# A post-norm attention and mixture-of-experts layer on one core: shared down products moved into the last part, a router in four column groups, two steps moved to ScalarE, and a new order

## What is computed

```python
Q, K, V = (x @ W.T).reshape(b, s, h, hd)                  # h = 16, hd = 16
scores = einsum('bshd,bstd->bsht', Q, K) / sqrt(hd)       # heads of one token
x = layernorm(x + (softmax(scores) @ V).reshape(b, s, dm) @ Wfc.T)
scores = sigmoid(x @ router_weight.T); sfc = scores + router_bias
# 4 groups of 8 experts: best 2 groups by the sum of their top 2, then top 4 experts
topk_w = 2.5 * scores[topk_idx] / sum(scores[topk_idx])
mixed = sum_k topk_w[k] * (silu(x @ gate_w[e].T) * (x @ up_w[e].T)) @ down_w[e].T
shared = (silu(x @ sg.T) * (x @ su.T)) @ sd.T
x = layernorm(x + mixed + shared)
```

## Time and profile before

| | us |
|---|---|
| median of 3 runs | 721.03 |
| lowest, highest | 717.69, 722.21 |
| the profiled execution | 726.36 |
| its span, first to last instruction | 724.6 |
| first part, until PE transposes the first expert rows | 419.63 |
| last matmul of the expert loop starts | 656.97 |
| first picked rows added | 667.98 |

### The profile page before, as it was taken

How to read it: one execution, slowest core, us unless ns; L and a number is a source line. 1 busy time by engine, 2 the same in 40 slices (tenths; PEclk the granted TensorE clock), 3 DMA queues, 4 the chain that set the end, 5 groups by cost and what they waited for, 6 DMA issues and landing times.

```text
span 724.6 us, 16286 instructions
## 1 busy us (share of the span) xinstructions
PE 605.9 (84%) x4916; PEld 453.4 (63%) x4917; DVE 392.5 (54%) x1286; ACT 265.5 (37%) x521; POOL 290.1 (40%) x300
## 2 busy tenths in 40 slices
PE   6899998888597947578747989999999999993994
PEld 2366676565264625456524678788878888882883
DVE  2044675568056625368545446566565666562774
ACT  2344345334142502322212135455444555541224
POOL 4000003425327071516574316565556655554122
PEclk9999999789598977969776999999999999997899
DMA  6999968757237135859821224455445444444996
GB/s 225 270 223 250 238 187 236 174 163 214 99 109 220 45 126 181 323 180 382 286 106 67 90 71 148 133 144 157 147 133 154 150 159 158 148 153 153 417 411 238
DMA packets 125804, 135.34 MB, mean 187 GB/s; under 512 B 76856, under 2 KB 107071, under 8 KB 125120
## 3 DMA queue, kind: packets, MB, share of 16 engines
q1 hardware_dynamic: 108288, 95.92, 45.3%
q0 software_dynamic: 12672, 34.10, 12.5%
q10 hardware_dynamic: 4800, 4.74, 1.9%
HBM read 74.79 MB, written 60.96 MB: 187 GB/s over the span
## 4 chain that ended last, share of the span: by engine, by line
PE 15%; SPq 12%; issue 11%; DVE 6%; DMA 5%; another core or an unknown queue 2%; DVEq 1%; ACT 1%; POOL 0%; POOLq 0%; ACTq 0%
PE bank L868 14%; SPq L468 7%; SPq L470 5%; DMA wgu_sb<-pick_rows 3%; DMA prod<-expert_rows 2%; PE bank L1241 1%; DMA pick_rows<-prod,ids 1%; DVE prod L1709 1%; DVEq L250 0%; DVE prod L1733 0%; DVE bidx L1456 0%; DVE best L1453 0%; DVE gtop L1426 0%; SPq L474 0%
## 5 line engine op out<-in xcount | busy, mean ns | idle before, releaser
L527 POOL DMA_INDIRECT expert_rows<-stage,pos x128 | 127.2, 993 | 150.4 <-DVE pos L1393 80.4
L561 POOL DMA_INDIRECT pick_rows<-prod,ids x136 | 136.5, 1004 | 119.0 <-issue 51.8
L868 PE MATMUL bank<-prod 128*128 128x128 f32 x1088 | 134.4, 277 | 2.5 <-issue 1.3
L868 PEld LDWEIGHTS bank<-prod 128*128 128x128 f32 x1088 | 126.8, 192 | 5.7 <-issue 3.3
L868 PE MATMUL bank<-wgu_sb 128*32 128x64 f32 x2048 | 80.2, 297 | 50.3 <-issue 35.0
L868 PEld LDWEIGHTS bank<-wgu_sb 128*32 128x32 f32 x2048 | 64.5, 139 | 72.9 <-issue 59.2
L868 PE MATMUL bank<-wd_sb,wqkv_sb 128*128 128x512 f32 x192 | 92.8, 628 | 6.0 <-DMA wqkv_sb<-in_wqkv 6.0
L1709 DVE COPY prod<-wgu_sb 128x512 f32 x136 | 61.2, 491 | 63.0 <-issue 38.6
L827 ACT ACTIVATE prod<-bank,kept 128x256 f32<-128x256 f32 x136 | 57.1, 471 | 40.4 <-PE bank L868 21.9
L868 PE MATMUL bank<-wd_sb,prod 128*128 x272 | 70.3, 381 | 1.3 <-issue 0.8
L868 PEld LDWEIGHTS bank<-wd_sb,wqkv_sb 128*128 128x128 f32 x192 | 37.2, 201 | 46.3 <-issue 40.2
(11 more groups left out here) (138 smaller groups left out, 777.0 us busy)
## 6 DMA issues: line engine op xcount, KB each, us to landing
prod<-expert_rows SPq DMA_DIRECT2D x136, 132.0 KB
wgu_sb<-pick_rows SPq DMA_DIRECT2D x32, 512.0 KB, 14.1
wgu_sb<-in_wgu SPq DMA_DIRECT2D x2, 2560.0 KB
expert_rows<-pad_rows SPq DMA_DIRECT2D x4, 1056.0 KB
wd_sb<-in_xT SPq DMA_DIRECT2D x8, 512.0 KB, 4.3
q_slots<-wd_sb SPq DMA_DIRECT2D x16, 256.0 KB
k_slots<-wd_sb SPq DMA_DIRECT2D x16, 256.0 KB
wgu_sb<-q_slots SPq DMA_DIRECT2D x16, 256.0 KB
```

The source lines that it names most:

```text
L527: pool.indirect_dma_start(xs, bass.IndirectOffsetOnAxis(ap=pos[e % 2][:, i, k:k + 1], axis=0), stage[:, i, k, :], None, bounds_check=XROWS ...
L561: pool.indirect_dma_start(z, bass.IndirectOffsetOnAxis(ap=ids[par][:, j:j + 1], axis=0), y_sb[par][:, j, :], None, bounds_check=TOPK * NTO ...
L868: return pe.matmul(dst, lhsT, rhs, start=(k == 0), stop=(k == n - 1))
```

## The change

1. **Shared down products of chunks 5, 6 and 7** are taken out of the first part. `DOWN_AT_ONCE = 5` chunks keep them. PE does the other three after the expert loop, straight into the banks of the last sums, where x1 (without the shared product) and the picks are added. The last sums take the chunks in the order 5, 6, 7, 0, 1, 2, 3, 4. Chunk 7's `hsT` gets a third place, over the projection weights. DVE does no `add_shared` for these three.
2. **The router** holds its weights (32 columns) still and streams 128 tokens, with the four tiles in four groups of 32 columns of the array. The result is transposed, so ACT copies it (`copy_logits`) and PE turns it back with one transpose (`turn_logits`).
3. **ACT normalises** the first layer norm (from a negated mean that DVE computes, `negate_mean`) and **copies the counts** (`copy_ranks`).
4. **All five lists** get a new order; in it, waits for banks move along.

```diff
-COUNT_BANKS = (4, 4, 4, 4, 5, 7, 4, 4)
-DOWN_BANKS = ((5, 4), (5, 4), (7, 4), (5, 4), (5, 4), (5, 4), (5, 4), (5, 4))
+COUNT_BANKS = (4, 4, 4, 4, 4, 4, 4, 5)
+DOWN_BANKS = ((5, 4), (5, 4), (5, 6), (5, 4), (5, 4))
+DOWN_AT_ONCE = 5
+LAST_ORDER = (5, 6, 7, 0, 1, 2, 3, 4)
...
+        hsT_last = wqkv_sb.rearrange("p k c -> p (k c)")[:, 0:2 * CT].rearrange("p (k c) -> p k c", k=2)
+
+        def hs_of(b):
+            return hsT[b % 2] if b < DOWN_AT_ONCE + 2 else hsT_last
...
+        logT = eneg1
...
-        ones_e = sb("ones_e", [P, NE])
+        ones_e = over(prod, 25 * DM - NE, NE)
...
-                    at = (g * TPC + t) * P
+                    at = (LAST_ORDER[g] * TPC + t) * P
...
             invert(0)
             invert(1)
-            scatter_rows(0, 0, 8)
+            scatter_rows(0, 0, 5)
             invert(2)
...
+            scatter_rows(3, 6, 16)
+            scatter_rows(4, 0, 8)
             invert(6)
-            scatter_rows(4, 14, 16)
-            scatter_rows(5, 0, 3)
+            scatter_rows(4, 8, 16)
+            scatter_rows(5, 0, 9)
             invert(7)
...
+            def copy_logits(b):
+                act.wait_ge(S["logT_ready"], b + 1)
+                if b:
+                    act.wait_ge(S["onehot_ready"], b)
+                act.activation(logT[:, :], banks[LOGITS_BANK][:, 0:P], ACT.Copy).then_inc(S["logT_copied"], 1)
+
+            def normalise(b):
+                act.wait_ge(S["rstd_ready"], b + 1)
+                act.wait_ge(S["nmean_ready"], b + 1)
+                for i in range(TPC):
+                    act.activation(x1_of(b)[:, i, :], res[:, i, :], ACT.Identity, bias=nmeant[:, i:i + 1],
+                                   scale=rstdt[:, i:i + 1]).then_inc(S["x1_ready"], 1)
+
+            def copy_ranks(e):
+                act.wait_ge(S["rank_ready"], e + 1)
+                if e:
+                    act.wait_ge(S["rk"], RK * e)
+                act.activation(ranks_sb[:, :, :],
+                               banks[COUNT_BANKS[e]][:, 0:(TPC + 1) * NE].rearrange("p (i e) -> p i e", e=NE),
+                               ACT.Copy).then_inc(S["rk"], 1)
...
-                for i in range(TPC):
-                    for k in range(KC):
-                        last = mm(banks[LOGITS_BANK][:, i * NE:(i + 1) * NE],
-                                  x1T_sb[b % X1T][:, k, i * P:(i + 1) * P], wr_sb[:, k, :], k, KC)
-                last.then_inc(S["logits_ready"], 1)
+                for k in range(KC):
+                    for i in range(TPC):
+                        last = mm(banks[LOGITS_BANK][i * NE:(i + 1) * NE, 0:P], wr_sb[:, k, :],
+                                  x1T_sb[b % X1T][:, k, i * P:(i + 1) * P], k, KC)
+                last.then_inc(S["logT_ready"], 1)
+
+            def turn_logits(b):
+                pe.wait_ge(S["logT_copied"], b + 1)
+                pe.transpose(banks[LOGITS_BANK][:, P:2 * P], logT[:, :], ident[:, :])\
+                    .then_inc(S["logits_ready"], 1)
...
-            def normalise(b):
+            def negate_mean(b):
                 dve.wait_ge(S["rstd_ready"], b + 1)
-                for i in range(TPC):
-                    dve.tensor_scalar(x1_of(b)[:, i, :], res[:, i, :], mvt[:, i, 0:1], rstdt[:, i:i + 1],
-                                      ALU.subtract, ALU.mult).then_inc(S["x1_ready"], 1)
+                dve.scalar_tensor_tensor(out=nmeant[:, :], in0=mvt[:, :, 0], scalar=-1.0, in1=rstdt[:, :],
+                                         op0=ALU.mult, op1=ALU.mult).then_inc(S["nmean_ready"], 1)
...
+            def sum_down(g, b):
+                pe.wait_ge(S["hs_ready"], 2 * (b + 1))
+                for t in range(TPC):
+                    for k in range(2):
+                        pe.matmul(sum_of(g, t), hs_of(b)[:, k, t * P:(t + 1) * P], wsd_sb[:, k, :],
+                                  start=(k == 0 and t % 2 == 0), stop=False)
...
+            for g in range(CH - DOWN_AT_ONCE):
+                sum_down(g, LAST_ORDER[g])
+            for g in range(CH):
+                sum_rows(g, LAST_ORDER[g])
```

More of the change, by code:

```diff
@@ new lines, in _ @@
+            stage_rows(1, range(3, 4))
+            evacuate(6, 2)
+            normalise(3)
+            copy_o(4, 1)
+            evacuate(6, 3)
+            exponents(5, 0)
+            turned(3, 0)
+            evacuate(6, 4)
+            expand(5, 0)
+            copy_ranks(2)
+            stage_rows(2, range(0, 1))
+            exponents(5, 1)
+            tanh_of(0, 0)
+            stage_rows(2, range(1, 2))
+            turned(3, 1)
+            expand(5, 1)
+            copy_logits(3)
@@ new lines, in _ @@
+            evacuate(6, 5)
+            sigmoid_parts(3)
+            stage_rows(2, range(2, 3))
+            copy_o(5, 0)
+            exponents(6, 0)
+            stage_rows(2, range(3, 4))
+            normalise(4)
+            copy_o(5, 1)
+            evacuate(7, 0)
+            expand(6, 0)
+            evacuate(7, 1)
+            evacuate(7, 2)
+            exponents(6, 1)
+            copy_ranks(3)
+            evacuate(7, 3)
+            stage_rows(3, range(0, 2))
+            expand(6, 1)
@@ L771, in _ @@
+            copy_o(6, 0)
+            stage_rows(3, range(2, 3))
+            turned(4, 0)
+            tanh_of(0, 1)
+            turned(4, 1)
+            copy_o(6, 1)
+            copy_logits(4)
+            stage_rows(3, range(3, 4))
+            sigmoid_parts(4)
+            evacuate(7, 4)
+            tanh_of(1, 0)
+            evacuate(7, 5)
+            normalise(5)
+            exponents(7, 0)
+            tanh_of(1, 1)
             turned(5, 0)
-            tanh_of(1, 1)
+            stage_rows(4, range(0, 3))
@@ L1548, in _ @@
             moments_of(4)
+            route(3, 0)
+            shift(6, 0)
+            negate_mean(4)
+            route(3, 1)
             weights(6, 0)
-            normalise(4)
+            route(3, 2)
+            shift(6, 1)
+            route(3, 3)
+            weights(6, 1)
+            place(3)
+            gated(0, 1)
             residual(5, 0)
```

776 lines of the change are left out of this document (363 added, 413 removed).

## The result

The changed kernel took 758.65 us (median of 4 runs, 756.54 to 763.28) against 720.33 us for the kernel before: a ratio of 1.054, with a 95% interval of 1.048 to 1.060. I had predicted 699.

A forecast was written before the change was run, and what follows sets the result against it. No engine total bounds the kernel; before the loop, latency and waits do, with most hanging on POOL's scatter chain. Terms -6.7, -8 and -7, the rest 0, sum to -21.7: 726.4 to 704.7, less 5.3 to the median, 699 us (690 to 709).

The forecast's parts named there:

- B: Rival, chance 0.10: before the loop, two more pairs of small-matmul batches held up by scatters, 16.6 us each; 733 us.
- Term 1: At the loop's start: without the shared down products in front, the loop begins on the first loaded rows, -6.7 us.
- Term 2: Between loop and sums: the moved down products fill PE's 10.63 us of idling, 0 us (-3 to +10).
- Term 3: Router in four column groups: PE's gain against an added transpose, copy and hand-overs, 0 us (-8 to +5).
- Term 4: Normalising and count copies moved from DVE to ACT in the first part: 0 us (-9 to +4).
- Terms 5 and 6: First part's new order: less PE work before chunk 4's counts, -8 us; chunk 6's earlier projection halves POOL's 12.65 us hole, -7.
- rival A: Rival, chance 0.22: the part before the loop keeps its pace, only the tail's 6.7 us is gained, 714 us.

The follow-up runs named there:

- e5: The changed kernel itself, unaltered, run in the quiet condition: 611.4 us, ratio 0.961 to the kernel before.
- e3: The kernel before with the changed kernel's places in SBUF and its three more semaphores, unused, no instruction added: 639.0 us, ratio 1.001.
- e17: The changed kernel with 32 more instructions that do nothing on VectorE, crawling condition: 761.2 us, ratio 1.044 to the kernel before.
- e18: The changed kernel with the shared down products back in front of the loop and 24 more do-nothing VectorE instructions, crawling: 766.0 us, ratio 1.050.
- e4: The kernel before with only the shared down products of chunks 5 to 7 moved behind the loop, and the sums' chunk order: 638.7 us, ratio 1.002.
- e9: The changed kernel with the shared down products of chunks 5 to 7 back in front of the loop: 608.1 us, ratio 0.958 to the kernel before.
- e8: The changed kernel with the old router back: 616.8 us, ratio 0.971 to the kernel before.
- e7: The changed kernel with normalising and the copy of the counts back on VectorE: 626.3 us, ratio 0.983 to the kernel before.

## Why the prediction was wrong

**The step that failed** is the sentence that the change "rewrites the order of the first part and touches the loop not at all, so the question is when the loop can begin". The loop was in my sum with a difference of nothing and no bound. It was +39.6 us in the comparison, and -9.7 us in the quiet condition (e5 against e3). No rival covered it either; B put the slower case into the head. The evidence to be cautious stood in my own rows: GpSimd's scatters held up streams of instructions without a releaser, and the loop has 136 of them. I had also looked only for what the trace called crawling in the head; two pauses of 3.3 and 3.5 us stood in the loop.

**Term 1** (-6.7, down products behind the loop). In the crawling condition it was right: the loop began on the first loaded rows and no longer on these products. From the last scatter's end to the first transposes it takes 5.6 us instead of 12.2, so 6.6 of the head's 8.3 us are this term, and e17 against e18 gives 4.5. In the quiet condition it is worth nothing: e4 and e9 show no gain in the medians, since there the products fit beside the last scatters and row loads.

**Term 2** (0, -3 to +10). Right: +1.4 us to the first sum. The granted clock was 0.98 instead of 0.88, but the sums took as long as before (+0.1), so the 3 us that I had allowed for it did not come.

**Term 3** (0, -8 to +5). The new router is worth -6.5 us (e8), inside its bounds.

**Term 4** (0, -9 to +4). In the quiet condition ScalarE's share is worth -8.7 us in the head (e7), at the end of the range. In the comparison it may have cost instead. ACT pauses there while GpSimd scatters, and now holds normalising and staging, on which GpSimd waits. ACT and POOL of the changed kernel, crawling:

```profile
301.03 0.28 ACT L664 ACTIVATE eneg<-bank 128x128 f32<-128x128 f32 x1 [2.15 <-PE bank L990]
...
313.84 0.97 POOL L534 DMA_INDIRECT expert_rows<-stage,pos  x1 [0.30 <-issue]
316.41 1.04 ACT L631 ACTIVATE wgu_sb<-bank 128x512 f32<-128x512 f32 x1 [15.10 <-remote]
317.77 2.05 ACT L651 ACTIVATE sx<-prod,nmeant,rstdt 128x256 f32<-128x256 f32 x4
...
324.82 0.20 ACT L612 ACTIVATE stage<-idw 128x8 f32<-128x8 f32 x1
324.83 0.97 POOL L534 DMA_INDIRECT expert_rows<-stage,pos  x1 [10.02 <-ACT stage L612]
```

ACT stands 15.1 us, resumes 1.6 us after the last scatter (313.84 + 0.97), works off one chunk's normalising and the staging, and GpSimd has waited 10.0 us. How much of it each moved step costs was not measured.

**Terms 5 and 6** (-8 and -7). The first came true where it was priced: chunk 4's first scatter starts at 285.77 instead of 293.83. Then it was lost. The holes of the earlier trace rows are there under other names:

```profile
303.60 1.04 POOL L527 TENSOR_TENSOR rstdt<-vepst,neg_half 128x4 f32<-128x4 f32 x1 [7.73 <-DVE vepst L1401]
...
354.40 0.97 POOL L534 DMA_INDIRECT expert_rows<-stage,pos  x1 [8.32 <-ACT stage L612]
...
383.60 0.97 POOL L534 DMA_INDIRECT expert_rows<-stage,pos  x1 [9.07 <-DVE pos L1457]
...
404.58 0.97 POOL L534 DMA_INDIRECT expert_rows<-stage,pos  x1 [0.30 <-issue]
```

The scatter that waits for the positions of chunk 7 starts at 383.6. I had written that 384 or later would mean rival A, and as to the head A is very nearly what happened. The last scatter starts 1.9 us earlier than before (404.58 against 406.46), not 15. In the quiet condition (e5) the same order leaves no hole over 3.6 us from 203.8 us on, and the last scatter comes 22.0 us earlier:

```profile
203.82 1.04 POOL L527 TENSOR_TENSOR rstdt<-vepst,neg_half 128x4 f32<-128x4 f32 x1 [2.62 <-DVE vepst L1401]
...
221.57 0.97 POOL L534 DMA_INDIRECT expert_rows<-stage,pos  x1 [3.58 <-DVE pos L1457]
...
307.10 0.97 POOL L534 DMA_INDIRECT expert_rows<-stage,pos  x1 [0.30 <-issue]
```

That the quiet head's 22 agrees with my sum of 21.7 is luck: my terms were read from crawling rows, and in the quiet condition term 1 was too large and terms 3 and 4 too small.

## What to carry to other kernels

A part that a change does not touch is not a part that keeps its time: where another engine's work beside it can stall instruction streams, and where a loop's code will move, give the loop a term of its own with bounds. Before crediting a gain or loss of one or two per cent in a kernel with a hot loop, move the loop by a few instructions that do nothing, on one engine at a time; here that alone was worth -11 and +5 us in the quiet condition and +42 in the crawling one (there from one execution on either side), as much as the parts of the change. And when a trace holds gaps without a releaser, do not hand an engine that has them a further step of the critical chain, and measure in another session before building on them.

## What the runs showed of the hardware

The same program took 638 or 720 us according to the condition of the chip, and one chip was seen in both. In the crawling condition streams of small matmuls beside GpSimd's indirect DMAs took 20.5 us instead of 3.75. ScalarE stood up to 15.9 us without a releaser in the changed kernel, and in the loop it resumed 0.60 to 0.83 us after the end of a scatter in each of 29 pauses; GpSimd's own scatters took 1.0 us each in both. In the quiet one a pass of the loop took 0.2 to 0.3 us more with VectorE's first loop instruction at 760 or 772 than at 728, 740 or 804.
